# A graph kernel's edge sort: each tile's destination base from a table, the record load moved to SyncE, and one transposition issued a step earlier in the first message stage

## The reference

```python
edge_index = jnp.stack([src, dst])
x = x + _L0_gnn_ref(h, edge_index, ...)                 # attention, softmax by source
x = x + _L1_gnn_ref(h, edge_attr_64, ..., src, dst)     # sum over edges of (descriptors @ Wdesc.T) * xj[dst], by src
x = x + _L2_gnn_ref(h, edge_index, edge_weight, ...)
x = x + _L3_gnn_ref(h, edge_index, edge_attr_3, edge_attr_50, ...)
```

## Time and profile before

| | |
|---|---|
| median of 3 runs | 9352.47 us (9346.34 to 9354.06) |
| the profiled execution, time | 9256.08 us |
| its span | 9254.4 us |
| busy: PE / DVE / ACT / POOL | 5371.4 / 4851.5 / 2716.0 / 4470.1 us |
| indirect DMAs of sort, first to last start | 332.3 to 1786.4 us |
| indirect DMAs of l1e, first to last start | 4107.0 to 5528.8 us |

### The profile page before, as it was taken

How to read it: one execution, slowest core, us unless ns; L and a number is a source line. 1 busy time by engine, 2 the same in 40 slices (tenths; PEclk the granted TensorE clock), 3 DMA queues, 4 the chain that set the end, 5 groups by cost and what they waited for, 6 DMA issues and landing times. The chain is left out here.

```text
span 9254.4 us, 143056 instructions
## 1 busy us (share of the span) xinstructions
PE 5371.4 (58%) x26415; PEld 4003.0 (43%) x26416; DVE 4851.5 (52%) x15866; ACT 2716.0 (29%) x7299; POOL 4470.1 (48%) x5261
## 2 busy tenths in 40 slices
PE   6777777504444446444445455566666635877775
PEld 4555555303333346424444441244444423555553
DVE  8555555343444446643333348556666644555556
ACT  2333333202222246440000015422323223333333
POOL 0355555536666666415555550056666502555553
PEclk9877777655555557655665557777777755666667
DMA  1233333511111134212222220022222201222221
GB/s 47 79 101 103 102 104 104 64 35 47 48 48 48 49 83 113 71 30 58 58 57 57 57 52 0 19 58 60 58 58 59 56 1 43 56 54 55 52 54 42
DMA packets 859247, 541.02 MB, mean 58 GB/s; under 512 B 652852, under 2 KB 758152, under 8 KB 858760
## 3 DMA queue, kind: packets, MB, share of 16 engines
q0 software_dynamic: 148032, 300.00, 11.9%
q1 hardware_dynamic: 609192, 192.51, 10.0%
q10 hardware_dynamic: 101920, 47.37, 2.0%
HBM read 411.68 MB, written 127.68 MB: 58 GB/s over the span
## 5 line engine op out<-in xcount | busy, mean ns | idle before, releaser
L1336 POOL DMA_INDIRECT l2e_rows<-l_rows,l2e_idx x832 | 846.0, 1017 | 1028.7 <-DVE l2e_idx L1344 769.2
L1336 POOL DMA_INDIRECT l3e_rows<-l_rows,l3e_idx x832 | 813.6, 978 | 932.6 <-DVE l3e_idx L1344 644.6
L1336 POOL DMA_INDIRECT l1e_rows<-l_rows,l1e_idx x832 | 796.9, 958 | 882.0 <-DVE l1e_idx L1344 606.4
L795 POOL DMA_INDIRECT src_records<-sort_rec,sort_idx x784 | 780.9, 996 | 742.7 <-DVEq L673 508.7
L1219 POOL DMA_INDIRECT dst_rows<-l0d_out,l0d_idx x832 | 814.3, 979 | 487.0 <-issue 255.2
L885 DVE TENSOR_TENSOR acc<-acc,l1e_pR 128x128 f32 x832 | 238.8, 287 | 899.8 <-DMA l0m_rows<-dst_rows 773.4
L1631 PE MATMUL l1e_pG<-k_weights,l1e_dT 64*128 64x128 f32 x1664 | 240.5, 436 | 708.0 <-ACT l1e_dT L1651 418.3
L2001 PE MATMUL l3e_pH<-l3e_dT,k_weights 50*128 50x256 f32 x832 | 388.7, 559 | 322.0 <-DMA run_ml<-h_nodes 299.0
L1183 PE MATMUL l0d_pT<-identb,l0d_oh 128*128 128x128 bf16 x832 | 125.7, 306 | 698.8 <-DVE l0d_oh L1164 420.0
L1631 PEld LDWEIGHTS l1e_pG<-k_weights,l1e_dT 64*128 64x128 f32 x1664 | 182.4, 301 | 784.8 <-issue 417.6
L1809 PE MATMUL l2e_pV<-l2e_rows,ident 128*128 128x512 f32 x416 | 329.8, 885 | 319.4 <-DMA l2e_rows<-l_rows,l2e_idx 263.9
(11 more groups left out here) (416 smaller groups left out, 14970.5 us busy)
## 6 DMA issues: line engine op xcount, KB each, us to landing
sort_rows<-lo_rows SPq DMA_DIRECT2D x196, 256.0 KB
sort_rec<-rec ACTq DMA_DIRECT2D x98, 472.0 KB
l0m_rows<-dst_rows SPq DMA_DIRECT2D x416, 66.0 KB, 2.0
l0m_rows<-dst_rows POOLq DMA_DIRECT2D x416, 66.0 KB
l1e_rec<-src_records SPq DMA_DIRECT2D x832, 32.0 KB
l2e_lrow<-dst_local SPq DMA_DIRECT2D x208, 128.0 KB
l3e_rec<-src_records SPq DMA_DIRECT2D x832, 25.0 KB
l0d_meta<-src_records SPq DMA_DIRECT2D x832, 6.0 KB
```

The source lines that it names most:

```text
L795: e.indirect_dma_start(kn.by_src_rec[:, :], bass.IndirectOffsetOnAxis(ap=r["idx"][:, st.quad, j:j + 1], axis=0), r["rec"][:, st.quad, j, : ...
L1336: e.indirect_dma_start(r["rows"][:, st.quad, j, 0:width], None, table[:, :], bass.IndirectOffsetOnAxis(ap=r["idx"][:, st.quad, j:j + 1], a ...
```

## The change

In front, the stationary operand of the matmul into `hd` is no longer all ones: it is a slice of `to_row` with a single column of ones, column i for group i. Row i of `hd` then holds the counts of group i alone. Offsets sums them by matmuls (`small`) and builds `tile_base`: for each group (row) and each of its 8 tiles the first destination place of every block, kept as two float16 parts, half of it rounded and the rest. In sort, `drank` becomes three matmuls: the counts within the tile, and two that take row i of the two parts, the stationary operand being column i of twice the identity and of the identity, read 128 times. `dbase`, `carry` and the wait for it are gone. `load_records` is issued by SP, with lag 1, behind `load_rows`. In l1e `mults` has lag 2 instead of 1 and `add` 4 instead of 3; `turn_rec` keeps 0.

```diff
@@ front, tensor
-                    e.matmul(r["hd"][:, 0:GT * NB], kn.onesh[:, :], r["hi"][:, i % 2, 0, :, :].rearrange("p t b -> p (t b)"),
+                    e.matmul(r["hd"][:, 0:GT * NB], r["to_row"][:, P - i:2 * P - i], r["hi"][:, i % 2, 0, :, :].rearrange("p t b -> p (t b)"),
                              start=(i == 0), stop=(i == n - 1), skip_group_check=True).then_inc(r["pe"], 1)
@@ offsets, tensor
+            e.wait_ge(r["grouped"], 1)
+            e.matmul(r["small"][:, 2 * NB:3 * NB], kn.before[:, :], r["group"][:, :], start=True, stop=True,
+                     skip_group_check=True)
+            e.matmul(r["small"][:, 3 * NB:4 * NB], kn.ones[:, :], r["group"][:, :], start=True, stop=True,
                      skip_group_check=True).then_inc(r["sums"], 1)
@@ offsets, vector
+            ch(e.tensor_tensor(r["row"][:, 0, :], r["small"][:, 2 * NB:3 * NB], r["excl"][:, 0:NB], ALU.add))
+            for t in range(GT - 1):
+                ch.wait()
+                ch(e.tensor_tensor(r["row"][:, t + 1, :], r["row"][:, t, :], counts[:, t, :], ALU.add))
+            ch.wait()
+            rows = r["row"][:, :, :].rearrange("p t b -> p (t b)")
+            ch(e.tensor_scalar(kn.tile_base[:, 0, :], rows, 0.5, None, ALU.mult))
+            ch.wait()
+            ch(e.scalar_tensor_tensor(kn.tile_base[:, 1, :], kn.tile_base[:, 0, :], -2.0, rows, ALU.mult, ALU.add))
             e.wait_ge(r["counted"], 2)
...
-            ch(e.tensor_copy(kn.base_dst[:, :], r["excl"][:, 0:NB]))
@@ sort, sync
+            def load_records(st):
+                wait_quad_free(e, r, "sent", st, GT)
+                e.dma_start(r["rec"][:, st.quad, :, 0:NREC], rec_tiles[:, bass.ds(st.i * GT, GT), :]
+                            ).then_inc(r[f"rec_ld{st.quad}"], 16)
+
             e.wait_ge(kn.low_st, 32)
-            run_steps(e, ch, [(load_rows, 0)], n)
+            e.wait_ge(r["cleared"], 1)
+            run_steps(e, ch, [(load_rows, 0), (load_records, 1)], n, 4)
@@ sort, vector, place
                 wait_step(e, r["dranked"], st)
-                e.wait_ge(r["carried"], st.i + 2)
@@ sort, scalar
-            run_steps(e, ch, [(load_records, 0), (wide_hot, 1), (low, 0), (keys, 2), (mask, 1), (carry, 2)], n, 4)
+            run_steps(e, ch, [(wide_hot, 1), (low, 0), (keys, 2), (mask, 1)], n, 4)
@@ sort, tensor
             def drank(st):
-                e.wait_ge(r["carried"], st.i + 1)
+                wait_step(e, r["hot"], st)
                 wait_step(e, r["dtaken"], st, 1)
-                e.matmul(r["drank"][:, 0:(GT + 1) * NB].rearrange("p (t b) -> p t b", b=NB), r["onerow"][0:1, :],
-                         r["dbase"][0:1, None, :].to_broadcast([1, GT + 1, NB]), start=True, stop=False,
-                         skip_group_check=True)
...
-                for j in range(GT):
-                    ins = e.matmul(r["drank"][:, (j + 1) * NB:(GT + 1) * NB].rearrange("p (t b) -> p t b", b=NB),
-                                   kn.onesh[:, :], r["ohhi"][:, st.quad, 0, j:j + 1, :].to_broadcast([P, GT - j, NB]),
-                                   start=False, stop=(j == GT - 1), skip_group_check=True)
+                out = r["drank"][:, 0:GT * NB]
+                e.matmul(out, kn.beforeh[:, :], r["ohhi"][:, st.quad, 0, :, :].rearrange("p t b -> p (t b)"),
+                         start=True, stop=False, skip_group_check=True)
+                for k, t in enumerate((kn.twiceh, kn.identh)):
+                    ins = e.matmul(out, t[:, bass.ds(st.i, 1)].to_broadcast([P, P]), kn.tile_base[:, k, :],
+                                   start=False, stop=(k == 1), skip_group_check=True)
@@ l1e, tensor
-            run_steps(e, ch, [(mults, 1), (add, 3), (turn_rec, 0)], STEPS, QUAD)
+            run_steps(e, ch, [(mults, 2), (add, 4), (turn_rec, 0)], STEPS, QUAD)
```

More of the change, by code:

```diff
@@ L249, in setup @@
     kn.first_at = sb("first_at", [P, NB], I32)
-    kn.tot_dst = sb("tot_dst", [P, NB])
 def node_buffers(kn, ctx):
@@ L308, in vector @@
             ch(e.tensor_copy(kn.identh[:, :], kn.ident[:, :]))
+            ch(e.tensor_scalar(kn.twiceh[:, :], kn.ident[:, :], 2.0, None, ALU.mult))
             ch(e.tensor_copy(kn.onesh[:, :], kn.ones[:, :]))
@@ L365, in vector @@
             e.memset(r["zero"][:, :], 0.0).then_inc(r["zero_ok"], 1)
+            ch(e.memset(r["to_row"][:, :], 0.0))
+            ch.wait()
+            ch(e.memset(r["to_row"][:, P:P + 1], 1.0))
+            ch.wait()
             def center():
@@ L412, in vector @@
             e.wait_ge(r["pe"], n)
-            ch(e.tensor_reduce(kn.tot_dst[:, :], r["hd"][:, 0:GT * NB].rearrange("p (t b) -> p b t", b=NB), AX, ALU.add))
+            ch(e.tensor_copy(kn.tile_counts[:, :], r["hd"][:, 0:GT * NB]))
             ch(e.tensor_copy(kn.count[:, 1, :], r["hs"][:, 0:NB]))
@@ L535, in vector @@
         def vector(e, ch):
+            counts = kn.tile_counts[:, :].rearrange("p (t b) -> p t b", b=NB)
+            e.tensor_reduce(r["group"][:, :], counts.rearrange("p t b -> p b t"), AX, ALU.add).then_inc(r["grouped"], 1)
             ch(e.tensor_scalar(r["none"][:, :], kn.count[:, 1, :], 0.0, None, ALU.is_equal))
@@ L541, in vector @@
             e.wait_ge(r["sums"], 1)
-            ch(e.tensor_copy(r["tot"][:, 0:NB], kn.tot_dst[:, :]))
+            ch(e.tensor_copy(r["tot"][:, 0:NB], r["small"][:, 3 * NB:4 * NB]))
             ch(e.tensor_copy(r["tot"][:, NB:2 * NB], r["small"][:, NB:2 * NB]))
@@ L593, in offsets @@
                       ("lt", [P, 2, nt, SLOTS], F32), ("b", [P, 2, SLOTS], F32),
-                      ("none", [P, NB], F32)],
-               sems=["sums", "iota", "less", "counted"])
+                      ("none", [P, NB], F32), ("group", [P, NB], F32), ("row", [P, GT, NB], F32)],
+               sems=["grouped", "sums", "iota", "less", "counted"])
 def sort(kn):
@@ L676, in scalar @@
         def scalar(e, ch):
-            def load_records(st):
-                wait_quad_free(e, r, "sent", st, GT)
-                e.dma_start(r["rec"][:, st.quad, :, 0:NREC], rec_tiles[:, bass.ds(st.i * GT, GT), :]
-                            ).then_inc(r[f"rec_ld{st.quad}"], 16)
             def low(st):
@@ L701, in mask @@
                 e.activation(r["mask"][:, st.par, 4:8, :], r["same"][:, 1, :, :], ACT.Relu).then_inc(r["masked"], 1)
-            def carry(st):
-                wait_step(e, r["dranked"], st)
-                e.activation(r["dbase"][0:1, :], r["drank"][0:1, GT * NB:], ACT.Copy).then_inc(r["carried"], 1)
             def keys(st):
```

22 lines of the change are left out of this document (10 added, 12 removed).

## The result

The changed kernel took 9426.68 us in the median of three runs (9413.91 to 9427.0) against 9352.47 us, a ratio of 1.0077 (95% interval 1.0054 to 1.0099). The forecast was 8984 us, 3.9% faster. In the profiled execution (span 9412.3 us) sort's indirect DMAs start over 1497.6 us instead of 1454.1, a step of (1497.6 - 9.4) / 97 = 15.3 us.

The account below looks back on a forecast made before the run. Sort was taken as bound by a loop of waits through ACT's record load and carry, l1e by PE's late results. Sort -260, l1e -114 and additions +6 made -368 us: 9352 to 8984 us, range 8820 to 9180.

Parts of the forecast that it names:

- Late results of PE: In sort and l1e, while POOL issues indirect DMAs, PE's results become usable 2.5 to 6 us late.
- part 4: In sort, POOL's 11.2 us bounds next; a step goes from 14.9 to 12.25 us, a gain of 260 us.
- 2 x (L + 1.6): In sort, four lookups a step through two halves of `sj`: 8.2 us with L = 2.5, 11.2 with L = 4.
- times 1.09: In sort, jitter on the 11.24 us floor, from layer 0's stage (6.15 us against 5.6), giving 12.25 us.
- my sign of being wrong: In sort, the forecast is wrong if `sort_prod` waits for PE for more than 4 us a step.
- Slower: In sort, L = 5.85 wins nothing; L = 7 makes a step 17.2 us, the kernel 9583 us; chance 0.04.
- Part 1: In sort, moving the record load to SP removes ACT's 8.98 us wait; the loop by `sent` becomes 6.8 us.
- only the issue is saved: In sort, ACT loses only 0.49 us of issuing a step: 48 us less, 9310 us; chance 0.03.
- Parts 2 and 3: In sort, dropping the carry ends DVE's 3.19 us idling; three matmuls for ten cut PE from 11.2 to about 9 us.
- Part 5: In l1e, `turn_rec` a step ahead of its product hides lateness: 6.85 to 6.3 us a step, 114 us less.
- l1e gains nothing: In l1e, DVE's sums wait for PE as long as before, only elsewhere: 9098 us; chance 0.17.
- Part 6: Added work in offsets, front and const, and sort's first broadcasts waiting 4.4 us for a memset: together 6 us.

Follow-up runs that it names:

- lookup loop: Micro kernel without the graph work: 256 PE lookups read by DVE, POOL issuing DMAs beside; on chip 5 1219 us with gathers, 171 and 172 with direct DMAs and SP loads.
- the table alone: Kernel before with only the base read from the table (three matmuls, no carry), record load left on ACT: 0.9999 on chip 2, 0.9962 on chip 3.
- fewer matmuls: One part of the attention table per sort lookup instead of three, on chip 5: 0.9963 in the kernel before, 1.0018 in the changed kernel.
- The run on chip 3: Kernel before with only the record load moved from ACT to SP, on chip 3: 0.9707, sort 1019.4 us.
- the first comparison: The whole changed kernel against the kernel before, on a chip where PE's results are late: 9426.68 against 9352.47 us, 1.0077.

## Why the prediction was wrong

**Where it failed.** The step is "Late results of PE" and what part 4 made of it: "a lookup's result comes L late", with the floor taken as the largest of POOL's 11.2 and 2 x (L + 1.6), times 1.09. I had read the earlier trace rows as a fixed delay that other work can cover. On a late chip it isn't fixed. In the lookup loop beside gathers it grew to 16.8 us for a lookup of six matmuls. In sort two thirds of DVE's unnamed waits (59 of 90) end only when POOL's burst has ended, and what DVE has left to do then stands behind the burst and not beside it: in the timeline above from 1018.67 to the next send at 1023.57, 5.05 us of POOL's idling on top of the 9.98 us of its eight DMAs. That is the step of 15 us in place of the forecast 12.25. The sum had only the lookups in it, too: DVE waited 246.1 us for `rank`, which stands in no term, and 120.1 for lookups. So my sign of being wrong, `sort_prod` waiting more than 4 us a step, didn't show (it was 2.4 us); the wait was at the other place. In the rival "Slower" I had written that results come on time when POOL is idle, and used it as the argument against.

That says why nothing was won in sort on a late chip; why some 50 us were lost there is not shown. Sort's bursts filled 980 to 995 us in every late run. The pauses between them summed to 461 us before, 452 in both other traces of the same sort code, 456 with the table alone and 428 with fewer matmuls. With the load on SP they were 507, with the table too 504 and 515, and 505 with fewer matmuls as well. The longer pauses go with the load's move in every run, and neither with the length of the bursts nor with the number of matmuls.

**Part by part.**

- Part 1: Right where nothing is late: ACT's wait closed the loop, and the load on SP alone is worth 2.9% (222 us), "only the issue is saved" (48 us) being far off. On a late chip the same edit gives 1.0019. That SP's broadcasts are covered "while a step is longer than 8 us" was wrong: at 10.4 us a step DVE waits for them 65 times between 600 and 1300 us, up to 3.2 us, which cost nothing only because POOL never stopped; on the late chip no such wait is seen. The Trainium skill ("Trainium Kernel Development and Optimization", Key Constraints) says that issuing DMAs from several engines only saves the sequencer's issue time. The run on chip 3 gained far more than that; the gain isn't in the DMAs but in ACT's other work, which no longer stands behind the load's wait.
- Parts 2 and 3: The carry's wait went, and PE's work fell (226.6 to 187.5 us in a window). Neither binds once the load is moved: 1017.5 us with both, 1019.4 without.
- Part 4: Without lateness a step is 10.4 us and not 12.25. Two terms were too large: the 0.89 us of handing over, since POOL goes from one send into the next, and the factor 1.09, which was itself lateness, taken from layer 0's stage, which takes 1057 us there and not 1277.
- Part 5: Wrong on every chip: POOL's issue of 5.04 us binds l1e where nothing is late. Where it is, PE's products wait for DVE instead of ACT, 552 us for 418, and the kernel with this order alone loses 0.35%. (The 785 us of the earlier trace rows add to these 418 us the waits of the weight loads, 367 us, which lie beside them, so the wait that I meant to remove was about half as long.) The rival "l1e gains nothing" was right on this stage.
- Part 6: The first send of sort starts 2 to 6 us later in the traces without lateness (332.8 before, 334.4 to 339.0 after), for 6 forecast, and 0.7 us later in the first comparison.

**The sum, where its premise holds.** Sort 229 us and l1e 0, less 5: 224 us, as between the two spans (7818.3 on chip 3 and 7593.1 on chip 6), 3.0%, against 368 us and 3.9%. The sign of the forecast depends on the chip.

**What stays open.** What makes PE's results late on some chips. Chips and hours changed together (2 and 5 earlier, 6, 3 and 4 later), so it may be the chip or its state. All executions compared here carry records of each instruction, and a start and an end record for each would fit two times 0.70 us, as would the 25 us by which the delay outlasted the gathers if records pile up; both are guesses. The Trainium skill ("NOTIFIC — the notification-queue block", section 7.1) says that this block holds its producers back rather than lose a record inside, and that such a stall would mean that the notification path throttled an engine. No run here shows that this is the cause. Nor is it shown how much of PE's work POOL's bursts hold up: by their recorded starts 5366 of sort's 7397 matmuls before, and 4077 of 6604 after, begin while a burst runs, so the two don't exclude each other. And why the load's move lengthens the pauses by some 50 us on a late chip is open.

## What to carry to other kernels

Where idle times end with nothing that the trace can name ("remote", "issue"), look whether they end with another engine's burst: then what follows the wait stands behind the burst, and the loop may not be costed as the largest of its parts. Removing a wait gains nothing if a second one, which ends at the same burst, stands right behind it. And time such a change on more than one chip: here one edit is 0.8% slower on one and 3.0% faster on another.

## What was not expected of the hardware

The same program takes 9216 to 9380 us on some chips and 7815 to 7831 us on others, 18 to 20% apart, nearly all of it in stages where POOL issues indirect DMAs (sort 1444 and 1247 us, l1e 1421 and 1047, layer 3 1390 and 1055), and almost none in the others (from the end of layer 0's stage to l1e's first gather 765 us on both). In the lookup loop on chip 5, beside a full stream of indirect DMAs, PE's results come at multiples of 0.70 us, 1.40 us on the mean for each of its instructions, and for some 25 us after the last gather still; beside POOL's direct DMAs and SP's loads nothing is late (171 and 172 us for 256 lookups).
